# A graph-and-attention layer: another order in its opening, a bias row from head sums on GpSimd, and graph layers on 1250 instead of 1280 columns

## What is computed

```python
x_norm = layer_norm(x, norm_g, norm_b)                       # of the already normalized x
out1 = gat_conv(x_norm, src, dst, W1, a_src1, a_dst1, b1, 4, 192, N)
out2 = gat_conv(out1,   src, dst, W2, a_src2, a_dst2, b2, 2, 96, N)
graph = concatenate([x, out2], -1) @ Wu + bu
# gat_conv: h = x @ W, one logit per edge from (h*a_src).sum and (h*a_dst).sum,
#           leaky_relu, softmax over the edges of a target, weighted sum of h[src]
k = elu(x @ Wk + bk) + 1 ; q = elu(x @ Wq + bq) + 1 ; v = x @ Wv + bv
attention = (q (k^T v)) / (q sum(k)) @ Wo + bo
x = x + graph + attention
x = x + mixture_of_8_experts(layer_norm(x))                  # best 2 of 8 for each row
```

## Time and profile before

| | us |
|---|---|
| median of 3 runs (lowest, highest) | 1038.85 (1037.54, 1039.32) |
| the profiled execution, as a whole | 1036.3 |
| its span, first to last instruction | 1034.6 |
| PE, DVE, ACT, POOL busy | 925.5, 754.5, 359.2, 118.7 |

### The profile page before, as it was taken

One profiled execution on the slowest core, in us unless ns is written; L12 is line 12 of the kernel. 1 busy time (PEld: TensorE's weight loads), 2 busy tenths in 40 slices (PEclk: granted clock), 3 DMA queues, 4 the chain that ended last, 5 costly groups with the idle time before them and its releaser, 6 DMA issues.

```text
span 1034.6 us, 17152 instructions
## 1 busy us (share of the span) xinstructions
PE 925.5 (89%) x6335; PEld 673.7 (65%) x6335; DVE 754.5 (73%) x1706; ACT 359.2 (35%) x475; POOL 118.7 (11%) x132
## 2 busy tenths in 40 slices
PE   5979999999888999989979999949888489999994
PEld 4846666666554655656769999838855356666662
DVE  6768789897766696986488999599979934444442
ACT  4841122122225332432334455205536433232320
POOL 4000000000001000000000000000010055545541
PEclk9989999999999999999989999978989689999998
DMA  9240222226441855637777100007055668778761
GB/s 278 91 168 18 76 78 77 62 99 255 139 173 65 304 178 181 204 111 237 244 316 307 51 1 1 1 1 320 2 208 206 226 195 200 194 178 191 187 168 21
DMA packets 61468, 155.44 MB, mean 150 GB/s; under 512 B 11957, under 2 KB 31287, under 8 KB 58443
## 3 DMA queue, kind: packets, MB, share of 16 engines
q1 hardware_dynamic: 48602, 112.33, 30.9%
q0 software_dynamic: 9936, 34.23, 13.3%
q10 hardware_dynamic: 2848, 7.77, 1.9%
HBM read 108.34 MB, written 48.94 MB: 152 GB/s over the span
## 4 chain that ended last, share of the span: by engine, by line
PE 70%; DVE 18%; issue 3%; DMA 3%; ACT 3%; DVEq 1%; SPq 1%; ACTq 0%; POOLq 0%
PE PS L1859 45%; PE PS L2129 14%; DVE arena L1596 3%; PE PS L1951 3%; DVE arena L1530 2%; PE PS L2290 2%; DVE arena L1524 2%; DVE arena L1318 1%; PE PS L2029 1%; PE PS L1962 1%; PE PS L1896 1%; DMA b2c<-in_L_gnn_b_dram 1%; PE PS L2305 1%; DVE arena L1317 1%; DMA arena<-in_L_ffn_W_dram 1%
## 5 line engine op out<-in xcount | busy, mean ns | idle before, releaser
L1859 PE MATMUL PS<-arena 128*128 128x384 f16 (+7 forms) x3396 | 568.2, 323 | 5.3 <-DVE arena L1849 3.0
L1859 PEld LDWEIGHTS PS<-arena 128*128 128x128 f16 (+2 forms) x3396 | 321.6, 99 | 214.6 <-issue 16.4
L2129 PE MATMUL PS<-arena 128*128 128x193 f32 (+1 forms) x1200 | 182.4, 314 | 11.6 <-DVE arena L1530 11.5
L2129 PEld LDWEIGHTS PS<-arena 128*128 128x128 f32 x1200 | 179.3, 193 | 14.8 <-DVE arena L1530 8.8
L1046 ACT ACTIVATE arena<-arena,AS 128x1280 f32<-128x1280 f32 x60 | 81.7, 1362 | 89.9 <-DVE arena L1524 89.5
L1530 DVE SCALAR_TENSOR_TENSOR arena<-arena 128x1280 f32<-128x1280 f32 x60 | 89.0, 1484 | 4.9 <-PE PS L2129 2.5
L1524 DVE SCALAR_TENSOR_TENSOR arena<-arena,AS 128x1280 f32<-128x1280 f32 x60 | 92.2, 1540 | 0.0
L1318 DVE TENSOR_SCALAR arena<-arena 128x240 f16<-128x240 f16 x324 | 88.7, 274 | 0.0
L1317 DVE TENSOR_SCALAR arena<-arena 128x128 f16<-128x128 f16 x324 | 79.7, 246 | 7.2 <-DMA b2c<-in_L_gnn_b_dram 7.2
L1848 DVE SCALAR_TENSOR_TENSOR arena<-PS,arena 128x768 f32<-128x768 f32 x27 | 25.8, 957 | 61.2 <-PE PS L1859 61.2
L1156 ACT ACTIVATE arena<-PS 128x1536 f16<-128x1536 f16 x27 | 39.2, 1451 | 75.4 <-PE PS L2290 75.4
(11 more groups left out here) (269 smaller groups left out, 898.3 us busy)
## 6 DMA issues: line engine op xcount, KB each, us to landing
arena<-in_L_ffn_W_dram SPq DMA_DIRECT2D x48, 384.0 KB, 3.9
fr_d<-arena SPq DMA_DIRECT2D x48, 384.0 KB, 3.7
arena<-fr_d SPq DMA_DIRECT2D x16, 1152.0 KB, 14.8
arena<-in_x_dram SPq DMA_DIRECT2D x18, 384.0 KB, 5.3
arena<-rr_d SPq DMA_DIRECT2D x4, 1280.0 KB, 8.1
g_d<-arena SPq DMA_DIRECT2D x10, 388.0 KB, 2.5
acc_d<-arena SPq DMA_DIRECT2D x10, 384.0 KB, 2.6
xf_d<-arena ACTq DMA_DIRECT2D x10, 384.0 KB, 3.2
```

The costliest lines, as they stand in the source:

```text
L1859: m = T.matmul(out, left[i][x], right[i][y], start=first and i + r == 0, stop=last and 3 * i + r == n - 1)
L2129: m = T.matmul(ps[sum_bank(h, b)][:, r * (C + 1):(r + 1) * (C + 1)], PT[i % deep][:, d * P:(d + 1) * P], feats, start=t == 0 and r == 0, s ...
```

## The change

The opening is reordered, one bias row is made in another way, and the graph layers stop at column 1250.

- **Loads.** SP starts with the edges; W1's first half comes behind them. Tile 2 of x stands ahead of Wk. The logit vectors are issued by ACT. norm_g, norm_b, b1 and layer 2's logit vectors move behind Wv; the last tile of x moves behind Wv too. VectorE blanks 3600 of the 6560 words of the count table that GpSimd blanked.
- **PE.** Four of M's twelve pieces, and the first turned tile, stand ahead of the read of `left`. `norm_bias` is gone from the loop. The key product of tile 0 stands between and behind the last two turned tiles, in banks 6 and 7.
- **Bias row.** GpSimd adds M's four heads (`msum`, 192 columns, two 128-row pieces at a time) and copies the eight logit columns; PE multiplies norm_b with these 200 columns behind the first value product, and b1's part is added in the same bank. VectorE's four additions are gone.
- **Wv's cuts** are made in the loop (ACT in tiles 7 to 9, DVE in tiles 8 and 9 and one behind it). The small loads are waited for later and each by its user.
- **Edges.** The 81 units are dealt to the steps 4 to 59 (FIRST = 4): none lies in tile 0.
- **Graph layers.** slopes, expo, weights and the maxima cover columns 0 to 1249; GpSimd sets the last 30 columns of the three PT buffers to 1 once.

```diff
-            w1_half(0, s_w1_in)
-            sp.wait_ge(s_edges_blank, 1)
+            sp.wait_ge(s_edges_ready, 1)
...
+            w1_half(0, s_w1_in)
             x_tile(0)
             w1_half(1, s_w1b_in)
             x_tile(1)
             sp.dma_start(W2A[:, :, 0:CW], ...)
+            x_tile(2)
+            weight(0, Wk)
+            for t in range(3, XS):
                 x_tile(t)
+            sp.wait_ge(s_const_ready, CONST)
+            sp.dma_start(xf_d[NP:NP + P, :], zrow).then_inc(s_xs_blank, 16)
+            for t in range(XS, NT - 1):
                 x_tile(t)
             sp.wait_ge(s_stage_low, CUTS)
             weight(1, Wv)
+            x_tile(NT - 1)
             sp.wait_ge(s_xn_ready, XS)
             sp.dma_start(bkrow, bk.partition_broadcast(P)).then_inc(s_bias_in, 16)
+            (nbc, b1c, ngc, a2c: the small columns, s_small_in)
...
+            for k in range(0, KC, 2):                      # GpSimd
+                pool.wait_ge(s_m_ready, 2 * k + 4)
+                g.tensor_copy(msum[:, k:k + 2, CW:]..., heads[:, :, :, CW:])
+                msum_step(g.tensor_tensor(total, heads[:, :, 0, 0:CW], heads[:, :, 1, 0:CW], ALU.add))
+                for h in range(2, H1):
+                    msum_step(g.tensor_tensor(total, total, heads[:, :, h, 0:CW], ALU.add))
...
-                if 4 <= t < 4 + CUTS:                      # ACT, loop over tiles
-                    high(0, t - 4)
+                if t < CUTS:
+                    high(0, t)
+                if t >= NT - CUTS:
+                    high(1, t - NT + CUTS)
...
+                if 1 <= t < 1 + CUTS:                      # DVE, end of the loop's body
+                    stage_low(0, t - 1)
+                if t > NT - CUTS:
+                    stage_low(1, t - 1 - NT + CUTS)
...
+                if t >= NT - 2:                            # PE, loop over tiles
+                    c = t - NT + 2
+                    i = product(ps[key_bank(0) + c][:, 0:HALF], xnt(0, P), cols(WK, c * HALF, (c + 1) * HALF))
...
-            return range(step * NU // DENSE, (step + 1) * NU // DENSE)
+            n = DENSE - FIRST
+            return range((step - FIRST) * NU // n, (step - FIRST + 1) * NU // n) if step >= FIRST else range(0)
...
-                V.scalar_tensor_tensor(PT[i % deep], BUF[:, unit % 3, :], 2.0, CT[:, t, 0:NP], ALU.min, ALU.mult)
+                V.scalar_tensor_tensor(PT[i % deep][:, 0:N], BUF[:, unit % 3, 0:N], 2.0, CT[:, t, 0:N], ALU.min, ALU.mult)
```

## The result

| | before | after | after, again, on another chip |
|---|---|---|---|
| median, us (lowest, highest, runs) | 1039.09 (1037.54, 1040.82, 4) | 1030.37 (1026.69, 1031.08, 4) | 1033.59 (1027.15, 1035.02, 7); before beside it 1038.55 |
| ratio to before, 95% interval | | 0.9911 [0.9887, 0.9935] | 0.9927 [0.9901, 0.9954] |
| the profiled execution: span | 1034.6 | 1024.9 | 1031.9 |
| start of K of tile 1 | 85.12 | 79.30 | 80.12 |
| from there to the last key bias | 129.3 | 132.8 | 132.6 |

The change makes the kernel 0.9% faster, 8.7 us (interval 6.8 to 11.7); 9.6 were forecast, 1029.3 against 1030.37. On the other chip the ratio gives 0.7%, and the medians lie 5.0 us apart. The table was read, to 0.1 us, from the first and last start of the lines that end each stage.

The account below looks back on a forecast made before the run. PE held 70% of the chain and DVE 18%, with the slack in the opening. Terms -6.3 (opening), -0.8 (bias row), +1.2 (keys and values), -1.8 (G), -1.9 (graph layers) gave -9.6: median 1029.3 us, range 1024.0 to 1037.0.

Parts of the forecast that it names:

- First transposes: Opening: with the edge loads ahead of W1, the first transpose moves from 6.47 to about 8.1 us (bounds 0 and +2.8).
- rival 1: GpSimd's additions hold VectorE's cuts, or (second cause) the first transposes come late by the full 2.8: 1032.9 us; chance 0.12.
- Read of `left`: Opening: four of M's pieces beside the read at full clock; third `normed` at 28.0 instead of 31.26, gain 3.3 us.
- Loop and the wait for the last tile: Opening: Wv issued near 43, VectorE waits some 4.6 us for x's last tile; K of tile 1 at 78.8, -6.3.
- Rival 2: Opening: the last tile of x doesn't make VectorE wait; V of tile 0 starts some 4.6 earlier: 1024.7 us; chance 0.10.
- Bias row: VectorE's three lost additions, ahead of PE's wait at 235.99, give -0.8 us; GpSimd's additions taken as 0, up to 3.6.
- Keys and values: Tiles 1 to 9 carry three more units of edges, hidden on VectorE: +1.2 us, up to 5.2 if not hidden.
- rival 3: VectorE becomes the bound of keys and values: three units cost 5.2, half-clock products 11.9; 1045.2 us; chance 0.11.
- G: Two more units, +0.8, and a wait and slow product removed in its eighth tile, -2.6: net -1.8 us.
- The two terms of the eighth tile: G: dealing one and two units removes the wait of 1.16 us and the slow product, 4.80 against 3.09: -2.6.
- Graph layers: 30 fewer columns: layer 2's maxima -0.7, its units -1.4, layer 1 nothing; sum given as -1.9 us.

Follow-up runs that it names:

- with W1 first: The changed kernel with the first half of W1 issued ahead of the four edge loads: 1030.12 us, ratio to before 0.9906.
- the run without the wait: The changed kernel with the last tile of x issued ahead of Wv instead of behind it: 1026.89 us, ratio to before 0.9867.
- The table of dealings: Units of edges dealt otherwise: changed kernel from tile 0 on, 0.9947; that with G's dealing kept, 0.9917; kernel before with G's dealing alone, 0.9963.
- FIRST = 2: The changed kernel with the units of edges dealt to 58 steps from tile 0's value products on, instead of 56 from tile 1: ratio to before 0.9947.
- G's dealing alone: The kernel before with only the dealing of units changed, G's 29 units placed as in the changed kernel: ratio to before 0.9963.

## Why the prediction was right, point by point

The sum was -9.6 and the profiled execution came out at -9.7. The mechanisms of the opening, G and the graph layers hold in the main; that the sum met the time so closely is luck. By stages it missed +2.3 in keys and values and +0.5 in the opening, and against that -1.4 in G and -1.4 in three stages for which it had no term.

- **First transposes: wrong in size.** 8.1 was taken, +2.8 the upper bound (9.3); 11.20 came, and 9.28 to 11.66 in the runs with this order. The loads were priced by issue alone; the transposes began 7.55 us behind the issue of W1's half instead of 5.67. This is rival 1's second cause; with W1 first, K of tile 1 came 2.2 to 3.0 earlier.
- **Read of `left`: right in gain, wrong in what sets the end.** `normed` was forecast at 28.0 and came at 28.24. But the step said that VectorE, leaving the branch as late as before, holds it. In the trace VectorE has the keys by 25.3 and then waits 1.00 us (at 27.45) for PE, whose order is M's pieces, first turned tile, keysT (26.97). PE, and so W1's landing, sets it, and an earlier W1 (24.51 in that run) moves it.
- **Loop and the wait for the last tile: right.** Wv at 43.85 (about 43), the tile at 54.7 (53.2), the wait 5.34 (4.6); V at 68.81 (66.7), two later because the first key half ran in part at half clock, 4.64, and the landing was late; then 10.49 to K of tile 1 (10.9 and 1.2 for the clock). -5.8 against -6.3. Rival 2 was the mirror of this and fell; its price, 4.6, is about what the run without the wait gained.
- **Bias row: undersized.** Zero was taken for GpSimd's additions; they cost about 1 us of the opening. The gain of the missing additions, 0.8, came as about 1.
- **Keys and values: the mis-sized term.** +1.2 was taken from a range up to 5.2; +3.5 came. Time line of PE in after, its waits in this stage (the kernel before has none from K of tile 1 on):

```profile
98.44 0.57 PE L1973 MATMUL PS<-arena 128*128 128x240 f16 x4 [0.29 <-DVE arena L1333]
...
176.89 0.57 PE L1973 MATMUL PS<-arena 128*128 128x240 f16 x4 [0.96 <-DVE arena L1333]
...
196.37 0.57 PE L1973 MATMUL PS<-arena 128*128 128x240 f16 x4 [0.48 <-DVE arena L1333]
```

1.73 us of waits, about 0.5 because the four matmuls ahead of each wait run to their end, 0.57 us, where others are followed after 0.40, and 1.2 for the units: 3.4. The argument was that key biases that wait for PE show room on VectorE. Seven of nine still wait in after (one for 0.20 us only), and yet PE waits too: inside one tile each waits for the other. In VectorE's queue the units stand behind the key bias, so the room ahead of it can't be spent on them; whether more than four buffers of one-hot matrices would help, no run shows. Part of rival 3's mechanism thus came, with 3.5 of its 5.2 us and without its half-clock products. That room lay elsewhere: ahead of the key bias of tile 1, where VectorE, with two units' one-hots made, has no more units:

```profile
85.76 1.02 DVE L1361 SCALAR_TENSOR_TENSOR arena<-PS,arena 128x384 f32<-128x384 f32 x2 [10.86 <-PE PS L1884]
```

- **G: right in mechanism, undersized.** -0.8 and -1.8 were taken together, -4.0 came. The two terms of the eighth tile, a wait of 1.16 and a product 1.7 longer, add up to 2.9 and not to the 2.6 that stands there. And only that tile's second wait was counted: PE's waits for one-hots in G add up to 7.06 us before (the 0.97 behind VectorE's additions among them) and to 4.10 in after, because the first waits of the eighth and ninth tiles shrank as well. The eighth tile's, before and then in after (the ninth's went from 1.33 to 0.93):

```profile
282.32 0.57 PE L1951 MATMUL PS<-arena 128*128 128x240 f16 x4 [1.33 <-DVE arena L1310]
```

```profile
279.37 0.57 PE L1973 MATMUL PS<-arena 128*128 128x240 f16 x4 [0.92 <-DVE arena L1333]
```

With the slow product gone (1.7) and two more units (0.8 the other way) that is about 3.9. The table of dealings settles that the places of the units do it. The slow product needn't follow a second wait: with `FIRST = 2` two tiles have one, of 1.17 and 1.16 us, and G ran at full clock throughout.
- **Graph layers: right.** -0.6 and -1.4, against -0.7 and -1.4, which add up to -2.1 where the sum has -1.9; layer 1 gave nothing.
- **What no term held.** -1.6, +1.1 and -0.9 in three stages, ahead of layer 1, layer 1 and the rest. The first and the last had another sign in the second run; of the first the clock is the main cause (PE's 1312 matmuls took 206.99 us at 0.99 in the kernel before), of the last the cause isn't known. Layer 1's came again as +1.0, but with G's dealing alone, where the graph layers are as before, it was +0.6 as well; its cause is open. A forecast of this kernel to 2 us therefore says little about its terms; the stages do.

Open stays why W1's landing varies, and which of PE's waits end in half clock.

## What to carry to other kernels

When a load is moved behind another, ask which engine reads it in order: one tile of x behind one weight held VectorE for 5.3 us, and with it ACT (4.80) and PE (4.27), and one moved line took that back. An engine's idle time at one point of a tile is not room for work that stands behind that point in its queue: bound the price of added work by the engine that makes its operands too, 1.74 us a unit and not only 0.40 (three units cost 3.5), unless a trace shows the operands lying ready. And where executions of one program differ by 8 us, compare stages in traces, since a median of a few runs can't see terms of 2 us.

## What the runs showed of the hardware

The same wait is followed by either clock level. Behind 2.81 us of waiting for the same cut, the same 36 matmuls took 6.01 us in after and 7.47 in its second run, and each level came again in other runs. The mean granted clock of 60 to 80 us was 0.98 and 0.89. The key half just ahead of the wait took 3.09 us in both, so the length of the wait doesn't decide alone. The Trainium skill ("TensorE: Matmul & The Clock Gate", Part 1) says that the number of matmuls that run at the lower clock at a kernel's start varies from run to run of one kernel; here the same is seen in the middle of one.

A load's landing varies by 2.4 us in one order of loads: with W1 behind the edges the first transposes began at 9.28 to 11.66 in eight runs, and at 6.81 to 6.88 in the three changed kernels where W1 went first.

One VectorE operation with a single input, the first on the edges, ended just behind a GpSimd blanking that it met: it took 2.59 us beside the long blanking, 1.46 beside the shorter one in after (5.81 to 7.27, the blanking until 6.98), and 0.53 in the run with W1 first, where the blanking was over. That isn't so of every operation: the cut beside the blankings that stood in for the additions took its 1.75 us. Time line of after, and then of the run with W1 first:

```profile
4.42 2.56 POOL L781 MEMSET arena<- 128x2960 f32 x1
...
5.81 1.46 DVE L1214 TENSOR_SCALAR arena<-arena 81x512 int32<-81x512 int32 x1
```

```profile
8.77 0.53 DVE L1214 TENSOR_SCALAR arena<-arena 81x512 int32<-81x512 int32 x1 [2.88 <-DMA arena<-in_dst_dram]
```
